# First group of an adaptive-norm attention and SwiGLU block: softmax denominators by quarters, v copied out ahead of k's last copies, and a Newton chain moved behind the row maximum

## The reference

```python
def _ada_rmsnorm(x, t, gamma_w, beta_w):
    gamma = (t @ gamma_w.T)[:, None, :]
    beta = (t @ beta_w.T)[:, None, :]
    return gamma * _rmsnorm(x) + beta
...
    q = split(x @ W_q.T)      # 16 heads of 16
    k = split(x @ W_k.T)
    v = split(x @ W_v.T)
    attn = jax.nn.softmax(scale * jnp.einsum('bnqd,bnkd->bnqk', q, k), axis=-1)
    o = jnp.einsum('bnqk,bnkd->bnqd', attn, v)
...
x = x + a_alpha * _attention(_ada_rmsnorm(x, t, attn_gamma_w, attn_beta_w), W_q, W_k, W_v, W_o)
x = x + f_alpha * _swiglu(_ada_rmsnorm(x, t, ffn_gamma_w, ffn_beta_w), gate_w, hidden_w, out_w, out_b)
...
out = (input - mean) * jax.lax.rsqrt(var + EPS) * weight + bias
out = out + tar_bias          # tanh of a linear map of cond_256
return out * weight + bias
```

## Time and profile before

| | |
|---|---|
| median of three runs | 500.49 us (500.06 to 501.43) |
| profiled execution, its own time | 501.54 us |
| span of the profiled execution | 499.7 us |
| TensorE busy | 477.0 us, 95% |
| VectorE busy | 376.3 us, 75% |
| GpSimd busy | 271.0 us, 54% |
| ScalarE busy | 241.5 us, 48% |

### The profile page before, as it was taken

The page is one execution under the profiler, slowest core; times in us unless marked ns, Lnnn a source line. Parts: engine busy times, 40 slices in busy tenths (PEclk is TensorE's granted clock), DMA queues, the critical chain, the costliest instruction groups (busy, mean ns, idle before and its releaser), DMA issues.

```text
span 499.7 us, 11696 instructions
## 1 busy us (share of the span) xinstructions
PE 477.0 (95%) x4452; PEld 401.8 (80%) x4452; DVE 376.3 (75%) x776; ACT 241.5 (48%) x355; POOL 271.0 (54%) x179
## 2 busy tenths in 40 slices
PE   7888899999999999999999999999999999999990
PEld 4767778898888988888888988798888978888890
DVE  5878676678866888767885888778896798595636
ACT  3775653337452654437562564537453476323230
POOL 3446465455467444864458445674438545626471
PEclk9889999999999999999999999999999999999996
DMA  7463056600833036400845027420634015500111
GB/s 194 148 187 125 1 149 156 104 2 0 237 83 86 1 100 152 117 30 0 204 82 114 0 65 187 102 45 0 178 89 132 0 28 143 129 1 13 31 65 63
DMA packets 36058, 44.21 MB, mean 88 GB/s; under 512 B 3136, under 2 KB 31040, under 8 KB 36032
## 3 DMA queue, kind: packets, MB, share of 16 engines
q1 hardware_dynamic: 36032, 43.85, 34.6%
HBM read 35.18 MB, written 4.47 MB: 79 GB/s over the span
## 4 chain that ended last, share of the span: by engine, by line
PE 83%; DVE 6%; POOL 4%; ACT 3%; DMA 1%; issue 1%; DVEq 0%; SPq 0%
PE banks L655 33%; PE banks L674 18%; PE banks L467 9%; PE banks L573 6%; PE banks L605 4%; PE banks L502 4%; PE banks L591 3%; PE banks L596 3%; PE banks L578 1%; PE banks L536 1%; PE banks L626 1%; POOL gh L1443 1%; ACT kpar L841 1%; POOL hs L1438 1%; DMA work_c<-xn 1%; DMA xtok<-x_in 1%
## 5 line engine op out<-in xcount | busy, mean ns | idle before, releaser
L655 PE MATMUL banks<-x2s,gh 128*128 128x512 f32 x768 | 190.5, 397 | 0.0
L655 PEld LDWEIGHTS banks<-x2s,gh 128*128 128x128 f32 x768 | 140.5, 188 | 30.3 <-ACT x2s L912 0.4
L1438 POOL TENSOR_TENSOR hs<-act_t,hs 128x512 fp32r<-128x512 f32 x64 | 82.2, 1285 | 144.1 <-ACT hs L893 110.9
L674 PE MATMUL banks<-wout,hs 128*128 128x256 f32 x768 | 104.6, 286 | 0.8 <-POOL hs L1438 0.8
L674 PEld LDWEIGHTS banks<-wout,hs 128*128 128x128 f32 x768 | 97.7, 188 | 6.2 <-POOL hs L1438 1.2
L893 ACT ACTIVATE hs<-act_t 128x512 fp32r<-128x512 f32 x64 | 40.3, 630 | 86.9 <-DVE act_t L1214 80.8
L1210 DVE SCALAR_TENSOR_TENSOR act_t<-act_t,banks 128x512 f32<-128x512 f32 x64 | 43.9, 686 | 44.5 <-ACT act_t L886 43.3
L886 ACT ACTIVATE act_t<-banks 128x512 f32<-128x512 f32 x64 | 38.3, 598 | 74.8 <-PE banks L655 71.6
L1161 DVE RECIPROCAL work_c<-banks 128x512 f32<-128x512 f32 x16 | 53.7, 3356 | 6.9 <-PE banks L591 6.9
L467 PE MATMUL banks<-xs,wqk 128*128 128x512 f32 x192 | 48.7, 403 | 2.5 <-POOL xs L1390 1.6
L1214 DVE SCALAR_TENSOR_TENSOR act_t<-act_t,banks 128x512 f32<-128x512 f32 x64 | 44.0, 688 | 5.5 <-PE banks L655 1.1
(11 more groups left out here) (118 smaller groups left out, 657.4 us busy)
## 6 DMA issues: line engine op xcount, KB each, us to landing
xtok<-x_in SPq DMA_DIRECT2D x8, 512.0 KB, 5.2
work_c<-xn SPq DMA_DIRECT2D x16, 256.0 KB, 3.6
xres<-x_in SPq DMA_DIRECT2D x8, 512.0 KB, 6.9
row_aa<-rows_dram SPq DMA_DIRECT2D x16, 256.0 KB, 6.7
row_af<-rows_dram SPq DMA_DIRECT2D x16, 256.0 KB, 7.3
row_b<-rows_dram SPq DMA_DIRECT2D x16, 256.0 KB, 6.4
shift<-rows_dram SPq DMA_DIRECT2D x16, 256.0 KB, 6.1
y<-final SPq DMA_DIRECT2D x7, 512.0 KB, 3.2
```

Source lines behind the costliest of these rows:

```text
L655: last = mm(banks[:, base + part, :], gh[:, a, k, w:w + P], x2s[:, b, k, :], start=(n == 0), stop=(n == 5))
L674: last = mm(banks[:, t // 2, D * (t % 2):D * (t % 2) + D], hs[:, c % 2, b, P * t:P * t + P], wout[:, a, c, :], start=(c == 0 and a == b an ...
L1438: tt(hs[:, c % 2, 1, :], act_t[:, c % 2, :], hs[:, c % 2, 0, :].bitcast(F32), ALU.subtract)\
```

## The change

All of it is in group 0. In attention, denominators are computed for 256 columns (four sequences) at a time, each as soon as the exponential of those sequences is there, into two banks; the reciprocals are taken by 256 columns too, and the values by quarters. The product with the values stays at 512 columns. On ScalarE keep_v stands ahead of par_k and place_v_swapped ahead of cut_hi(3), and cut_hi(5) behind the first o_split. On VectorE setup_weights comes ahead of the second x's sums of squares, and its rsqrt chain behind negate_max. On GpSimd the scaling of the second x, which waits for that chain, stands behind cut_lo(2), and the first o_split ahead of cut_lo(5). The idle-time products are 2 and 5 between the maxima (2 and 2 before) and 10 ahead of the output projection (16 before).

```diff
-WARM_LOADS, WARM_MAX, WARM_OUTPUT, WARM_NORM = 3, 2, 16, 4
+WARM_LOADS, WARM_LAST_MAX, WARM_MAX, WARM_OUTPUT, WARM_NORM = 3, 2, 5, 10, 4
+HALF = TOK // 2
+FIRST_O = (6, 1)
...
+            def first_sums(h, part):
+
+                pe.wait_ge(p_ready, 2 * h + part + 1)
+                if h and part:
+                    pe.wait_ge(o_steps, 1)
+                elif h:
+                    pe.wait_ge(recip_first, 1)
+                for j in range(J):
+                    last = mm(banks[32 * j:32 * j + 32, 0 if part else 7, quarter(part)], cst[:, C_BLK:C_BLK + 32],
+                              pt[:, 4 * part:4 * part + 4, j, :], start=True, stop=True)
+                last.then_inc(den_mm if part else den_first, 1)
+
+            def first_values(h, part):
+
+                if h == 0:
+                    pe.wait_ge(v_ready, 4)
+                for b in range(4 * part, 4 * part + 4):
+                    for j in range(J):
+                        last = mm(banks[32 * j:32 * j + 32, FIRST_O[h], L * b:L * b + L], vblk[:, b, J * h + j],
+                                  pt[:, b, j, :], start=True, stop=True)
+                last.then_inc(o_mm if part else o_first, 1)
...
-                pe.wait_ge(k_ready, 4)
-                warm_up(wqk[:, 0, 0], WARM_MAX, 5)
+                pe.wait_ge(v_out, 1)
+                warm_up(wqk[:, 0, 0], WARM_LAST_MAX, 7)
                 scores_for_max(0, 3)
-                warm_up(wqk[:, 0, 0], WARM_MAX, 5)
+                warm_up(wqk[:, 0, 0], WARM_MAX, 7)
...
-                for n in range(3):
-                    scores(0, n)
-                attend(0, 0)
+                scores(0, 0)
+                scores(0, 1)
+                first_sums(0, 0)
+                first_values(0, 0)
+                first_sums(0, 1)
+                scores(0, 2)
+                first_values(0, 1)
                 scores(0, 3)
-                attend(0, 1)
+                for part in range(2):
+                    first_sums(1, part)
+                    first_values(1, part)
...
-                if n >= 2 or later(g):
+                if not later(g) and n == 2:
+                    act.wait_ge(o_first, 1)
+                elif n >= 2 or later(g):
...
+                keep_v(0)
                 par_k()
-                keep_v(0)
...
+                place_v_swapped(0)
                 cut_hi(3)
-                place_v_swapped(0)
...
+                o_split(0, 0)
                 cut_hi(5)
-                o_split(0, 0)
+                o_split(0, 1)
                 cut_hi(6)
-                o_split(0, 1)
...
+            def first_normalise(h):
+
+                if h == 0:
+                    dve.wait_ge(v_ready, 4)
+                else:
+                    dve.wait_ge(o_steps, 2)
+                a, b = quarter(0), quarter(1)
+                dve.wait_ge(den_first, h + 1)
+                V.reciprocal(work_c[:, 0, a], banks[:, 7, a]).then_inc(recip_first, 1)
+                dve.wait_ge(den_mm, h + 1)
+                V.reciprocal(work_c[:, 0, b], banks[:, 0, b]).then_inc(o_steps, 1)
+                dve.wait_ge(recip_first, h + 1)
+                dve.wait_ge(o_steps, 2 * h + 1)
+                dve.wait_ge(o_mm, h + 1)
+                if h:
+                    dve.wait_ge(o_hi, 1)
+                    dve.wait_ge(o_lo, 1)
+                V.tensor_tensor(work_c[:, 1, :], banks[:, FIRST_O[h], :], work_c[:, 0, :], ALU.mult).then_inc(o_steps, 1)
...
                 setup_rows()
+                setup_weights()
                 dve.wait_ge(stage_lo, 1)
                 stats_x(1, x2n)
-                dve.wait_ge(x_stats, XS * 2)
-                rsqrt_both(1)
                 q_out(0)
                 for n in range(4):
                     max_over_keys(0, n)
                 negate_max(0)
-                setup_weights()
-                normalise(0, 0)
-                normalise(0, 1)
+                dve.wait_ge(x_stats, XS * 2)
+                rsqrt_both(1)
+                first_normalise(0)
+                first_normalise(1)
...
+                pool.wait_ge(x_stats, XS * 2)
+                finish_shift()
+                cut_lo(2)
                 pool.wait_ge(norm1_steps, RS * 2)
                 tt(xtok[:, :, :], xtok[:, :, :], nt1[:, 1, 0, :].unsqueeze(2).to_broadcast([P, TT, D]),
                    ALU.mult).then_inc(xs_scaled, 1)
-                finish_shift()
-                cut_lo(2)
                 cut_lo(3)
                 cut_lo(4)
+                o_split(0, 0)
                 cut_lo(5)
-                o_split(0, 0)
                 o_split(0, 1)
```

More of the change, by code:

```diff
@@ L185, in build @@
             sem, ("x2_kept", "x3_steps", "ln_stats", "ln_mean", "ln_scaled", "final_steps"))
+        den_first, o_first, recip_first = map(sem, ("den_first", "o_first", "recip_first"))
         last_dve, last_pool = sem("last_dve"), sem("last_pool")
@@ L233, in bank_of_st, with quarter @@
             return (4, 6, 4, 2)[n] if later(g) else 4 - 2 * (n % 2)
-        def banks_of_o(g, h):
-            return (0, 1) if h and not later(g) else (6, 7)
+        def quarter(part):
+            return slice(HALF * part, HALF * part + HALF)
         def bank_of_v(g):
@@ L584, in attend @@
                 pe.wait_ge(p_ready, 4 * g + 2 * h + 2)
-                o_bank, den_bank = banks_of_o(g, h)
-                if h and later(g):
+                o_bank, den_bank = 6, 7
+                if h:
                     pe.wait_ge(o_steps, 4 * g + 2)
```

## The result

The changed kernel takes 497.48 us (median of six runs, 497.29 to 497.67). The kernel before took 500.27 us in the same comparison (499.86 to 501.67). The ratio is 0.9933, with a 95% interval of 0.9914 to 0.9952. The forecast was 497.5, and 2.8 us were gained where 3.0 were predicted. By the lowest runs the gain is 2.6 us. In two later comparisons on other chips it is 3.4 and 3.8 us by the medians, 2.7 and 2.4 by the lowest runs, so that the median of before is the less steady of the two sides.

A forecast was written before the change was run, and what follows sets the result against it. Bound: group 0's late chain that TensorE waits for, ending with x's low part at 51.29 us. At 48.3 it saves 3.0: profiled 501.54 becomes 498.5, less 1.05 for the median gives 497.5; range 496.7 to 499.3.

The forecast's parts named there:

- The path and the total: Group 0, from v's copy to x's low part: it ends at 48.3 against 51.29 us, 3.0 us earlier.
- first quarter's sums: TensorE, denominators behind the first exponential: by quarters half the old time, 0.45 us, done at 32.7.
- The 3.0: End of x's low part on GpSimd, 48.3 against 51.29 us; everything behind it should move along.
- v's order: ScalarE, keep_v ahead of kpar's copies, cut_hi(3) behind the landing: of 1.8 us gained on v, 0.85 are left.
- Quarters: Group 0's attention: 256-column reciprocals 1.70 us, half of 3.36; denominators and values by quarters 0.45 each.
- Newton chain: VectorE, ten small steps moved behind the maximum from a wait for q's projection to 29.08, ending near 31.85.
- The held step: VectorE's Newton chain: one step, both operands in SBUF, held by GpSimd's cut_lo(2) to about 30.15, about 0.9 us long.
- GpSimd's floor: GpSimd's operations in a row from 31.9 us, without any wait, cannot end before 48.1.
- both limits: End of x's low part: 48.3 us by the chain, 48.1 by GpSimd's operations without any wait.
- The clock: Rival, chance 0.22: TensorE's clock falls at 30 us, gain 2.0 (498.5), or one stretch later, gain 1.2 (499.3).
- the three products between maximum and transposes: TensorE, warm-ups between the maxima from 2 and 2 to 2 and 5: said to speak for full clock, no size.

The follow-up runs named there:

- 2, 5 and 16: Changed kernel with 16 idle-time products ahead of the output projection in place of 10, still 2 and 5 between the maxima: 497.50 us.
- the two profiles at full clock: Changed kernel, and the kernel before with only its Newton chain moved (500.20 us): x's low part ends 19.7 and 22.1 us behind negmax.
- Old v order: Changed kernel with keep_v behind par_k and cut_hi(3) ahead of place_v_swapped again: 498.73 us.
- halves: Changed kernel with group 0's attention by halves again, denominators and reciprocals of 512 columns: 498.91 us.
- the early chain: Changed kernel with the Newton chain ahead of q's copy on VectorE and GpSimd's scaling of the second x ahead of the shift rows: 498.73 us.
- 2, 2, 10: Changed kernel with 2 and 2 idle-time products between the maxima in place of 2 and 5, and 10 ahead of the output projection: 499.46 us.
- 2, 2, 16: Changed kernel with the idle-time products of before, 2 and 2 between the maxima and 16 ahead of the output projection: 499.17 us.

## Why the prediction was right, and where its sizes were off

**The path and the total.** The landmarks, each measured from negmax (28.79 in the forecast, 28.93 in the profile of 2, 5 and 16, which shared the first fall): first exponential 2.4 predicted, 2.4 measured; first reciprocal 4.0 and 4.2; last product's end 12.8 and 13.1; x's low part 19.5 and 19.8. The step that fell short is the first quarter's sums: its reciprocal starts 0.8 us behind the start of its denominators (33.16 and 32.36 in that profile), where half of the old time gave 0.5. All later landmarks keep this distance of about 0.25 us.

The near hit of the total, 2.8 for 3.0, is in part luck. The 3.0 were read against a profile with two falls of the clock. The lowest runs gain 2.4 to 2.7 us, near the 2.4 of the two profiles at full clock; the medians gain 2.8, 3.4 and 3.8, depending on how many long executions of before are among the runs. Taken back one at a time, the three parts cost 1.1, 1.3 and 1.1 us by the medians, 0.9, 1.2 and 0.8 by the lowest runs; the latter add up to 2.8, for a gain of 2.7 on that chip.

**v's order: right.** The exponential moved by 0.84 us for 0.85; the rest of the 1.1 came from a transfer, as shown. The copy lands 4.3 us behind keep_v (4.36 forecast), the cut of 1.06 stands behind it (1.04), and kpar is hidden.

**Quarters: right in kind, too large in size.** The prediction gave them no sum of their own. From its times it would be 12.5 - 10.4 = 2.1; measured are 12.5 - 10.7 = 1.8 against the same profile, and 1.3 at full clock, since the 12.5 of before contained scores at the lower level.

**Newton chain: the step was mis-sized.** "From a stretch where VectorE then waited for the q projection" was true of the profiled execution, in which that projection ran partly at 1.2 GHz. At full clock q's projection ends at 19.4, and the chain ahead of the copy costs 1.1 us in the changed kernel. It was counted as zero. In before it cost 0.15 us at the lowest run; why so much less is not shown.

**The held step: right but for its kind.** The chain lost 0.56 us to GpSimd's cut, where some 0.7 were reckoned (one step "about 0.9 long", it was 0.73). But the step held has one operand and not two, so "with both operands in SBUF" is too narrow. The Trainium skill (SBUF — State Buffer, section "Who interferes with whom") also names tensor_scalar among the operations that can take the shared pair, when they run in a mode that uses both ports. The row of the held step agrees; which mode it ran in no run shows.

**GpSimd's floor: not the bound.** The prediction had both limits within 0.2 us of each other. Old v order, halves and the early chain each moved the end by at least their full delay, and 1.85 us less work on GpSimd gained nothing.

**The clock: the rival was real, its price nearly exact.** "gain 2.0" in place of 3.0 if it falls at 30 us; the measured loss is 0.96, and the gain left is 1.7. Its chance of 0.22 was fair for the changed kernel: of its 18 runs two stood 1.3 us or more above the median, and no profile tells where the clock fell in them. The prediction counted the three products between maximum and transposes as speaking for full clock, but gave them no price: with 2 and 2 in their place the median is 1.6 to 1.9 us higher, in twelve runs of each of two kernels. Nor did it see that before pays in most executions: its mean granted clock is 0.981 to 0.989 in 66 of 73 runs, that of the changed kernel 0.990 to 0.992 in 16 of 18, and its median of 501.45 stands 1.7 us above its lowest run. The first fall of its profile, at 15 us, lies ahead of any changed instruction.

**The rest of the program.** All behind the k projection moved along: from 47.39 in place of 51.34, 3.95 us, to 3.9 us in the span.

## What to carry to other kernels

Before two profiles are subtracted, lay them over each other at the last event ahead of the change and compare the granted clock up to there: here 1.2 of 3.95 us were no effect of the edit. Do the same behind it: 0.4 of the rest was a fall in the old profile. An operation that is hidden behind a matmul at the lower clock is not hidden in the executions at full clock, so look for what its cover would be then. Idle-time products are judged by the spread of many runs and not by the median of a few or by one profile. An idle engine's time is free only if nobody else is held by the work that is put there.

## What the runs showed of the hardware

- A VectorE step on eight columns with one SBUF operand (tensor_scalar) was held by GpSimd's running operation for 0.56 us; a sum of squares with its operand twice was held for 2.2 us.
- TensorE stopped for 2.46 and 1.58 us without a wait in the program, in both profiles of before with v's order alone, at the same place, and in no other profile. In these two a packet of the instruction queue came at 40.4 and 38.0 us, in the twelve others by 36.2. Its cause stays open, since no run was made on it.
- Six profiles have a TensorE wait of 1.2 us for the maxima. The lower level followed in four of them (before; before with v's order, with 16 and with 10 products; 2, 2, 10) and did not in two (before with the Newton chain moved; 2, 2, 16). With three more products the wait is 0.51 us in seven profiles, and none of them has the fall. The eighth kernel with these products, of the early Newton chain, has it at 26 to 29 us, behind waits of 0.66 us and more.
